# A second set of buffers for turned activations in a routed MLP, with their low parts taken from PSUM

## The reference, cut to what matters

```python
def _gemma_mlp(x, gate_w, up_w, down_w):
    g = jnp.einsum('bsh,hi->bsi', x, gate_w)
    u = jnp.einsum('bsh,hi->bsi', x, up_w)
    return jnp.einsum('bsi,ih->bsh', jax.nn.gelu(g, approximate=True) * u, down_w)
...
w, sel = jax.lax.top_k(rw, TOP_K)
w = w / w.sum(axis=-1, keepdims=True)
...
def step(acc, params):
    g, u, d, we = params
    return (acc + we[:, None, None] * _gemma_mlp(x, g, u, d), None)
...
x = x + _L0_cond_ref(...)   # experts (256 -> 1024 -> 256) plus the shared MLP
x = x + _L1_cond_ref(...)   # matrix mixed per batch
x = x + _L2_cond_ref(...)   # base and low rank
x = x + _L3_cond_ref(...)   # one of eight SiLU experts per batch
```

## Time and profile before

| what | value |
|---|---|
| time, median of 3 runs | 1183.42 us (1175.74 to 1189.4) |
| profiled execution, its own time | 1179.37 us |
| its span | 1177.8 us |
| TensorE busy (PE) | 1132.1 us, 96% |
| TensorE weight loads (PEld) | 954.0 us, 81% |
| VectorE (DVE) | 752.6 us, 64% |
| GpSimd (POOL) | 471.6 us, 40% |
| ScalarE (ACT) | 431.1 us, 37% |
| granted TensorE clock, mean | 0.993 of full speed |

### The profile page before, as it was taken

The page is one execution under the profiler, slowest core; times in us unless marked ns, Lnnn a source line. Parts: engine busy times, 40 slices in busy tenths (PEclk is TensorE's granted clock), DMA queues, the critical chain, the costliest instruction groups (busy, mean ns, idle before and its releaser), DMA issues.

```text
span 1177.8 us, 25073 instructions
## 1 busy us (share of the span) xinstructions
PE 1132.1 (96%) x6894; PEld 954.0 (81%) x6895; DVE 752.6 (64%) x1255; ACT 431.1 (37%) x845; POOL 471.6 (40%) x296
## 2 busy tenths in 40 slices
PE   8999999999999999899999999979999999899998
PEld 7999997777776877678777777879999999678876
DVE  6775677768767677696867776645555555444443
ACT  5355632232322322223222222322333232566664
POOL 3277588206337045080735481010000001888840
PEclk9999999999999999999999999989999999999999
DMA  7279768878678777888778886557544546667753
GB/s 222 53 253 322 285 202 265 256 209 260 201 203 278 237 208 207 242 240 270 216 215 248 243 260 185 155 161 187 141 135 134 135 133 237 195 209 244 222 164 94
DMA packets 257126, 245.07 MB, mean 208 GB/s; under 512 B 89216, under 2 KB 216448, under 8 KB 254976
## 3 DMA queue, kind: packets, MB, share of 16 engines
q1 hardware_dynamic: 243344, 193.95, 55.2%
q0 software_dynamic: 13680, 49.81, 13.9%
HBM read 176.59 MB, written 67.11 MB: 207 GB/s over the span
## 4 chain that ended last, share of the span: by engine, by line
PE 74%; DMA 8%; DVE 6%; SPq 5%; issue 5%; ACT 1%; POOL 1%; DVEq 0%; ACTq 0%; POOLq 0%
PE bank L774 12%; PE bank L775 11%; PE bank L776 11%; PE bank L1211 7%; PE bank L864 7%; DMA routing<-squares 6%; PE bank L1240 3%; PE bank L795 2%; DVE RS L1847 2%; PE bank L1052 2%; PE bank L863 2%; PE bank L915 2%; PE bank L1189 2%; PE bank L917 2%; PE bank L916 2%
## 5 line engine op out<-in xcount | busy, mean ns | idle before, releaser
L620 POOL TENSOR_TENSOR W<-raw,one 128x1024 fp32r<-128x1024 f32 x79 | 150.9, 1910 | 543.5 <-DVE acc L1914 254.0
L774 PE MATMUL bank<-W,RS 128*128 (+1 forms) x512 | 205.8, 402 | 6.3 <-DVE FS L1834 1.9
L864 PE MATMUL bank<-W,RS 128*128 x480 | 184.9, 407 | 19.4 <-DVE RS L1847 17.2
L622 POOL TENSOR_TENSOR W<-raw,W 128x1024 fp32r<-128x1024 f32 x79 | 200.9, 2543 | 6.2
L775 PE MATMUL bank<-W,RS 128*128 (+1 forms) x512 | 201.2, 393 | 0.0
L776 PE MATMUL bank<-W,RS 128*128 (+1 forms) x512 | 200.5, 392 | 0.0
L1301 ACT ACTIVATE FS<-bank 128x512 f32<-128x512 f32 (+1 forms) x200 | 115.0, 575 | 191.5 <-PE bank L776 180.7
L1847 DVE TENSOR_TENSOR RS<-routing,RS 128x512 fp32r<-128x512 f32 x120 | 134.6, 1122 | 64.6 <-ACT RS L1315 64.2
L1315 ACT ACTIVATE RS<-routing 128x512 fp32r<-128x512 f32 x120 | 75.7, 631 | 240.9 <-DMA routing<-squares 235.8
L1834 DVE TENSOR_TENSOR FS<-bank,FS 128x512 f32<-128x512 f32 (+1 forms) x136 | 88.8, 653 | 68.9 <-ACT FS L1301 46.9
L774 PE MATMUL bank<-RS,W 128*128 128x256 f32 x448 | 130.5, 291 | 1.0 <-DVE RS L1807 1.0
(11 more groups left out here) (236 smaller groups left out, 2052.9 us busy)
## 6 DMA issues: line engine op xcount, KB each, us to landing
raw<-in_w POOLq DMA_DIRECT2D x87, 512.0 KB, 5.2
acc<-in_w SPq DMA_DIRECT2D x70, 512.0 KB, 5.1
routing<-squares SPq DMA_DIRECT2D x120, 256.0 KB, 3.6
mixes<-acc SPq DMA_DIRECT2D x16, 1024.0 KB, 6.0
W<-mixes SPq DMA_DIRECT2D x16, 1024.0 KB, 6.1
squares<-X SPq DMA_DIRECT2D x60, 256.0 KB, 2.7
squares<-acc SPq DMA_DIRECT2D x60, 256.0 KB, 4.5
FS<-in_xT SPq DMA_DIRECT2D x200, 64.0 KB, 3.2
```

Source lines behind the costliest of these rows:

```text
L620: pool.tensor_tensor(hi, raw[:, k, :], ones_like(PIECE), ALU.mult).then_inc(done, 1)
L622: pool.tensor_tensor(lo, raw[:, k, :], hi.bitcast(F32), ALU.subtract).then_inc(done, 1)
L774: pe.matmul(ps, ah, bh, start=(i == 0), stop=False)
L864: mm = pe.matmul(both, chunk(hh[h], c), w2_, start=(h == 0 and c == 0), stop=(h == 1 and c == 3))
```

## The change

`hidT` gets two sets, one for even groups (`p = 0`) in the columns of `hid`, one for odd groups where it was. So that `hid` is free in this stage, the product of gelu and up is written over gelu (`gl`), and gelu waits for the transpose of the group before. ScalarE copies each turned half twice, first to the PSUM bank `turn_ps[h]`, then to the high part; VectorE's low part reads the bank instead of `hidT`. In the mixed groups the low part is still copied from `hidT`. On SyncE the read of half 0 goes ahead of the store of group `s-2`; the waits for low parts ahead of two reads go. Of the mixed weights of the second half, piece 0 was loaded at position 6 (in the place of the store that isn't there) and the pieces 1 to 5 at the positions 7 to 11; now pieces 0 and 1 are both loaded at position 7. The order of the last groups is changed in the same way.

```diff
-        hidT = [routing[:, I0 // 2 * h:I0 // 2 * (h + 1)] for h in range(2)]
+        hidT = [hid, [routing[:, I0 // 2 * h:I0 // 2 * (h + 1)] for h in range(2)]]
...
-        hidT_in = [sem(f"hidT_in{h}") for h in range(2)]
+        hidT_in = [[sem(f"hidT_in{p}{h}") for h in range(2)] for p in range(2)]
...
             def read_hidT(s, p, h, at):
 
                 n = P if at.half is None else S
                 sp.wait_ge(square_out[h], 16 * s + 16)
-                sp.dma_start(hidT[h].rearrange("p (a x) -> p a x", a=4)[:, :, 0:n],
+                sp.dma_start(hidT[p][h].rearrange("p (a x) -> p a x", a=4)[:, :, 0:n],
                              squares[p, h].rearrange("(a i) (g x) -> (i g) a x", a=4, g=4)[:, :, 0:n])\
-                    .then_inc(hidT_in[h], 16)
+                    .then_inc(hidT_in[p][h], 16)
...
-            sp.wait_ge(hl_done, 2 * S0 + 1)
             read_hidT(1, 1, 0, FIRST_TWO[1])
             with sp.Fori(0, NMIXED0) as m:
                 for k in range(BODY):
...
                     elif HALVES[0] + 3 <= k < HALVES[0] + 8:
-                        load_mixed0(m, 1, (k - HALVES[0] - 2,), S0 + BODY * m + HALVES[0] + 3)
+                        load_mixed0(m, 1, ((0, 1), (2,), (3,), (4,), (5,))[k - HALVES[0] - 3],
+                                    S0 + BODY * m + HALVES[0] + 3)
                     write_square(s, p, 1, at)
+                    read_hidT(s, p, 0, at)
                     if place_at(m, k - 2).half != 0:
                         store_chosen(S0 + s - 2, p, place_at(m, k - 2))
-                    else:
-                        load_mixed0(m, 1, (0,), S0 + BODY * m + HALVES[0] + 3)
-                    read_hidT(s, p, 0, at)
...
-            store_chosen(S1 - 3, 1, place(NR0 - 3))
-            read_hidT(NR0 - 1, 1, 0, LAST_TWO[1])
-            sp.wait_ge(hl_done, 2 * S1 - 2)
-            read_hidT(NR0 - 1, 1, 1, LAST_TWO[1])
+            read_hidT(NR0 - 1, 1, 0, LAST_TWO[1])
+            read_hidT(NR0 - 1, 1, 1, LAST_TWO[1])
+            store_chosen(S1 - 3, 1, place(NR0 - 3))
...
             def gelu(h, n2, first=False, n=512, squares=None):
                 act.wait_ge(gate_done, n2 + 1)
-                if not first:
+                if squares is not None:
+                    act.wait_ge(squared, squares)
+                elif not first:
                     act.wait_ge(hid_done, n2 - 1)
...
-            def hidden_hi_chosen(s, h, at):
+            def hidden_hi_chosen(s, p, h, at):
 
-                act.wait_ge(hidT_in[h], 16 * s + 16)
+                act.wait_ge(hidT_in[p][h], 8 * (s - p) + 16)
                 act.wait_ge(down_done, 2 * (S0 + s) + h - 1)
                 if at.half is None:
-                    act.activation(by_chunk(hh[h]), turned_hid(h), ACT.Copy).then_inc(hh_done, 1)
+                    act.activation(by_chunk(turn_ps[h][:, :]), turned_hid(p, h), ACT.Copy)
+                    act.activation(by_chunk(hh[h]), turned_hid(p, h), ACT.Copy).then_inc(hh_done, 1)
...
             def hidden_chosen(s, h, at):
...
-                if isinstance(s, int) and s == 0:
-                    dve.wait_ge(hl_done, n2 - 1)
-                else:
-                    dve.wait_ge(squared, 2 * s + h - 1)
-                TT(hid[h][:, 0:n], up_ps[h][:, 0:n], gl[h][:, 0:n], ALU.mult).then_inc(hid_done, 1)
+                TT(gl[h][:, 0:n], up_ps[h][:, 0:n], gl[h][:, 0:n], ALU.mult).then_inc(hid_done, 1)
...
-                dve.transpose(square[h][:, 0:n], hid[h][:, 0:n]).then_inc(squared, 1)
+                dve.transpose(square[h][:, 0:n], gl[h][:, 0:n]).then_inc(squared, 1)
 
-            def hidden_lo_chosen(s, h, at):
+            def hidden_lo_chosen(s, p, h, at):
                 dve.wait_ge(hh_done, 2 * (S0 + s) + h + 1)
                 if at.half is None:
-                    TT(by_chunk(hl[h]), turned_hid(h), by_chunk(hh[h].bitcast(F32)), ALU.subtract).then_inc(hl_done, 1)
+                    TT(hl[h], turn_ps[h][:, :], hh[h].bitcast(F32), ALU.subtract).then_inc(hl_done, 1)
...
-            hidden_late(0, 0, squares=2 * NR0 - 1)
-            hidden_lo_chosen(NR0 - 1, 0, LAST_TWO[1])
+            hidden_late(0, 0, lows=2 * S1 - 2)
+            hidden_lo_chosen(NR0 - 1, 1, 0, LAST_TWO[1])
```

More of the change, by code:

```diff
@@ L297, in by_chunk, with turned_hid, turned_mixed @@
             return t.rearrange("p (k a t) -> p k a t", k=4, a=4)
[L299 to L305, removed]
+        def turned_hid(p, h):
+            return hidT[p][h].rearrange("p (a k t) -> p k a t", a=4, k=4)
+        def turned_mixed(p, h, c):
+            return hidT[p][h].rearrange("p (a x) -> p a x", a=4)[:, :, 32 * c:32 * (c + 1)]
         block = ctx.enter_context(nc.Block())
@@ L477, in _ @@
             write_square(NR0 - 2, 0, 1, LAST_TWO[0])
+            read_hidT(NR0 - 2, 0, 0, LAST_TWO[0])
             load_late(0, (1,))
             store_chosen(S1 - 4, 0, place(NR0 - 4))
-            read_hidT(NR0 - 2, 0, 0, LAST_TWO[0])
             write_square(NR0 - 1, 1, 0, LAST_TWO[1])
@@ L1295, in split_x, with gelu @@
                 act.activation(xh[xset][p], xraw[p], ACT.Copy).then_inc(xh_done, 1)
-            def gelu(h, n2, first=False, n=512):
+            def gelu(h, n2, first=False, n=512, squares=None):
                 act.wait_ge(gate_done, n2 + 1)
-                if not first:
+                if squares is not None:
+                    act.wait_ge(squared, squares)
+                elif not first:
                     act.wait_ge(hid_done, n2 - 1)
@@ L1368, in chosen_group @@
                 g, n = S0 + s, 512 if at.half is None else D
-                gelu(0, 2 * g, n=n)
+                gelu(0, 2 * g, n=n, squares=None if isinstance(s, int) and s == 0 else 2 * s - 1)
                 if before_at is None:
@@ L1376, in chosen_group @@
                     split_x(g + 1, 1 - p, free=2 * g, mixed=after_at.half is not None)
-                gelu(1, 2 * g + 1, n=n)
+                gelu(1, 2 * g + 1, n=n, squares=None if isinstance(s, int) and s == 0 else 2 * s)
                 if before_at is not None:
                     for h in range(2):
-                        hidden_hi_chosen(s - 1, h, before_at)
+                        hidden_hi_chosen(s - 1, 1 - p, h, before_at)
             def group(g, p, n=3, after=1, xset=1):
@@ L1429, in hi, with gelu_late @@
                 act.activation(dst, src, ACT.Copy).then_inc(done, 1)
-            def gelu_late(k, q):
-                gelu(q % 2, 2 * (S1 + 2 * k) + q)
+            def gelu_late(k, q, squares=None):
+                gelu(q % 2, 2 * (S1 + 2 * k) + q, squares=squares)
             def hidden_hi_late(k, q):
@@ L1458, in ranks_hi @@
                         .then_inc(rh_done, 1)
[L1460 to L1463, removed]
+            gelu_late(0, 0, squares=2 * NR0 - 1)
+            hidden_hi_chosen(NR0 - 1, 1, 0, LAST_TWO[1])
+            gelu_late(0, 1, squares=2 * NR0)
+            hidden_hi_chosen(NR0 - 1, 1, 1, LAST_TWO[1])
             hidden_hi_late(0, 0)
@@ L1807, in split_x, with hidden @@
                 TT(xl[xset][p], xraw[p], xh[xset][p].bitcast(F32), ALU.subtract).then_inc(xl_done, 1)
-            def hidden(h, n2, turned=None, squares=None):
+            def hidden(h, n2, turned=None, lows=None):
                 dve.wait_ge(gelu_done, n2 + 1)
@@ L1814, in hidden @@
                     dve.wait_ge(turn_done, turned)
-                elif squares is not None:
-                    dve.wait_ge(squared, squares)
+                elif lows is not None:
+                    dve.wait_ge(hl_done, lows)
                 elif not (isinstance(n2, int) and n2 < 2):
@@ L1841, in hidden_squares @@
                     dve.wait_ge(square_out[h], 16 * s)
-                dve.transpose(square[h][:, 0:n], hid[h][:, 0:n]).then_inc(squared, 1)
-            def hidden_lo_chosen(s, h, at):
+                dve.transpose(square[h][:, 0:n], gl[h][:, 0:n]).then_inc(squared, 1)
+            def hidden_lo_chosen(s, p, h, at):
                 dve.wait_ge(hh_done, 2 * (S0 + s) + h + 1)
                 if at.half is None:
-                    TT(by_chunk(hl[h]), turned_hid(h), by_chunk(hh[h].bitcast(F32)), ALU.subtract).then_inc(hl_done, 1)
+                    TT(hl[h], turn_ps[h][:, :], hh[h].bitcast(F32), ALU.subtract).then_inc(hl_done, 1)
                 else:
-                    dve.tensor_copy(hm[h][:, P:D].rearrange("p (a t) -> p a t", a=4), turned_mixed(h, 1))\
+                    dve.tensor_copy(hm[h][:, P:D].rearrange("p (a t) -> p a t", a=4), turned_mixed(p, h, 1))\
                         .then_inc(hl_done, 1)
@@ L1937, in chosen_group @@
                     return
-                hidden_lo_chosen(s - 1, 0, before_at)
+                hidden_lo_chosen(s - 1, 1 - p, 0, before_at)
                 if add_at is not None:
                     add(g - 2, p, add_at)
-                hidden_lo_chosen(s - 1, 1, before_at)
+                hidden_lo_chosen(s - 1, 1 - p, 1, before_at)
             def group(g, p, n=3, after=1, xset=1, between=None):
```

(12 more changed lines are left out.)

2 lines of the change are left out of this document (1 added, 1 removed).

## The result

The changed kernel takes 1162.9 us, the kernel before 1181.4 (medians of 16 runs each): ratio 0.9839, 95% interval 0.9817 to 0.9860. That is 18.5 us, where I had forecast 8.3; the range of 1157 to 1189 holds the time, but the gain is more than twice the forecast. The profiled execution of the changed kernel took 1162.0 us.

A forecast was written before the change was run, and what follows sets the result against it. TensorE's waits in the routed stage, some 21 us plus what the clock loses, were taken as the bound; -8 - 2.3 + 0 + 2 = -8.3 us gave 1171.1 from the profiled execution or 1175.1 from the median, forecast 1174, range 1157 to 1189.

The forecast's parts named there:

- What bounds the kernel: TensorE is busy 96% of the span; some 21 us of its waits in the routed stage are all there is to win.
- The clock behind the bursts: Half-rate clock after the late down products behind position 0's two loads: 4 us taken for all four bursts.
- Low part from PSUM, -8: VectorE's low part beside GpSimd falls from 1.44 to 0.68 us by reading a bank: -8 us, bounds 0 to -10.
- kind (b): Ten or so TensorE waits of 0.4 to 1.1 us where GpSimd splits weights, 7 us in all.
- At a burst, -2.3: Ring position 0, two 512 KB loads ahead of a write: earlier read and quicker low part give -2.3 us, bounds +2 and -15.
- The first burst: First of four position 0 bursts: read lands some 1.5 us earlier, low part 1.4 quicker, copy 0.6 more: -2.3 of 2.99 us.
- rival B: The early read also removes the bursts' waits and the clock never falls: -21 us, 1162; chance 0.2.
- The rule cited there: At a burst: descriptors of one queue start in order, so a read cannot overtake the 1 MB and the gain stays small.
- The moved load, +2: Ring position 7 loads two pieces, a second burst per turn: costs 2 us in sum, bounds 0 and +16.
- The extra copy, 0 in clean groups: ScalarE's added copy makes each high part 0.6 us later, hidden in clean groups: 0, or 20 us if that cover were gone.
- A: The second burst, at position 7, behaves like the first: +11 us, 1194; chance 0.15.
- C: No change: VectorE's relief goes into waits for ScalarE, whose pair of copies is 0.6 us later: 1183; chance 0.12.

The follow-up runs named there:

- the fourth experiment: The changed kernel with the second half's first weight piece loaded at ring position 6 again and one piece at each of positions 7 to 11: 1157.6 us, 0.9822.
- the second: The kernel before plus the PSUM part alone (ScalarE copies to the bank, the low part reads it; one buffer set, old order): 1170.2 us, 0.9922.

## Why the prediction was wrong

*What bounds the kernel.* Right: 16.3 of the 17.4 us came from the routed stage. The clock behind the bursts was worth a little more than the 4 us I took: three falls of 3.4 us at half clock, 5.1 us (an estimate).

*Low part from PSUM, -8.* The size was right: 9 us alone (0.9922), and the duration to 0.01 us (0.69 beside GpSimd, forecast 0.68). Its place was not, so that the right size is in part luck. I had it take away the small waits of kind (b); they are 11.6 us of stopped time before, 12.3 with the PSUM part alone. VectorE's other operation with two SBUF inputs, L1807, became the late one (1.1 to 5.2 us), and the gain showed behind the bursts (15.5 to 11.3). I had named L1807 as still slow and had not asked what waits for it.

*At a burst, -2.3.* This is the step that failed: the early read brought 0.9 points, some 10 us. The first burst came out as forecast, -2.3 of 2.99: it waits 0.77. The others did not: I gave them 0, 0 and -0.6 us, and the waits of 2.64, 2.13 and 3.27 us became 0.26, 0.49 and 0.17, though the third restart got the wait of 2.64 at 603.28 in front of its burst. I worked the burst out with the write fixed at 332.52 and asked how much sooner the read could land behind it, at most 0.8 us. But the write's own time hung on SyncE's row of issues, and that on the pause at the loop's restart, 4.2 us between two issues that stand next to each other in the timeline. A read that goes out while SyncE would wait anyway, and not as the last issue ahead of the pause, makes all later ones earlier. In the changed kernel the write goes out 8.1 us ahead of the up product's last matmul (331.52 and 339.66), in the kernel before 6.7 us (332.52 and 339.26). 1.4 us of lead, where a transfer behind 1 MB needs 5.5 to 7, is the difference between no wait and 2.6 us with a fallen clock. I had given this 0.2 as rival B, with its 21 us, but for the wrong reason, and had put against it that the transpose waits for another transfer: that transfer moved too.

*The rule cited there.* The Trainium skill, "DMA: Bandwidth & Descriptors", section "Two DMAs through the same engine are not ordered", says that the descriptors of one queue start in order. The traces show landings, not starts, and nothing against it: what waited for the write and for the read began at 339.52 and 340.52 before, at 337.13 and 337.86 after. It was used on a time of issue that was not fixed.

*The moved load, +2.* Measured 0.17 points in the loop (0.9839 against 0.9822) and -0.1 with the loop written out (0.9772 against 0.9781); within the intervals both are 0, and so is 2 us.

*The extra copy, 0 in clean groups.* Not shown right: a further 0.6 us costs 12 us. What the first copy costs wasn't measured by itself; the 9 us of the PSUM part are what is left after paying it. The clean group of the earlier trace rows was one with slack; I take it that the groups beside loads, the majority, have little, but no run separates them.

*Rivals.* A fell with the fourth experiment, C with the second. B came nearest in time (1162), and had the bursts and the clock right but for the one wait and the one fall that stayed; its small waits stayed too, so its sum of 21 us is nearer than its parts.

## What to carry to other kernels

A queue that issues in order has a clock of its own: before working out what an earlier transfer brings, look for the longest gap between two of its issues, and ask what moves with it. Here the loop's restart costs SyncE 4 to 6 us, which nothing shows until the next burst meets it; writing the loop out gave 16 us, nearly as much as a rebuilt buffer scheme. And an engine at 42% is not free if its work stands between a landing and the operation that the bound engine waits for: price it by adding it once more.

## What the runs showed that I had not expected

The pause itself: 4.2 to 5.1 us on SyncE at the three restarts of a loop whose body holds 16 groups, 3.8 to 6.4 in the changed kernel, 0.7 to 1.2 where the loop is written out. The Trainium skill, "Runtime: NRT & Kernel Launch", section "Instruction fetch mechanics", says that a taken branch to code outside of what has been fetched stalls the engine until that code arrives. The direction agrees: in the chain above the 3.13 us lie between two instructions of the loop's own line. The runs show the pause and its worth, not what SyncE does in it.

Less work, slower: with GpSimd's splits cut away the changed kernel stands at 0.9900 instead of 0.9839. Its loads then come in a heap and the small transfers next to them land after up to 10 us; that this is the cause is read from the trace, and no run tests it.
